# Scaling the attention probabilities with two-tensor products on VectorE, the inverse row sum repeated along the columns

## The reference, cut to what matters

```
q = einsum('bsd,hed->bhse', x, W_Q);  k, v likewise
scores = einsum('bhse,bhme->bhsm', q, k) * scale
scores = where(causal, -1e9, scores)
pattern = softmax(scores, axis=-1)
z = einsum('bhsm,bhme->bhse', pattern, v)
out = einsum('bhse,hde->bsd', z, W_O)
```

## Time and profile before

| | |
|---|---|
| time, median of 3 runs | 1674.98 us (1674.21 to 1677.10) |
| the profiled execution, its time | 1677.12 us |
| its span (first to last instruction) | 1675.2 us |
| TensorE busy | 1617.7 us, 97% |
| VectorE busy | 1140.4 us, 68% |
| ScalarE busy | 767.0 us, 46% |
| GpSimd busy | 627.3 us, 37% |
| TensorE's granted clock | 0.995 of full speed |

### The profile page before, as it was taken

One profiled execution on the slowest core, in us unless ns is written; L12 is line 12 of the kernel. 1 busy time (PEld: TensorE's weight loads), 2 busy tenths in 40 slices (PEclk: granted clock), 3 DMA queues, 4 the chain that ended last, 5 costly groups with the idle time before them and its releaser, 6 DMA issues.

```text
span 1675.2 us, 29756 instructions
## 1 busy us (share of the span) xinstructions
PE 1617.7 (97%) x9992; PEld 1414.1 (84%) x9992; DVE 1140.4 (68%) x2889; ACT 767.0 (46%) x1897; POOL 627.3 (37%) x379
## 2 busy tenths in 40 slices
PE   7999999999999889999999999999999999999997
PEld 6988888898888878888888888888888888888886
DVE  5878878787887765556567578748784857753633
ACT  5666666665665543435333444335333533323221
POOL 2322223232222004323467225841675147533232
PEclk9999999999999999999999999999999999999999
DMA  6434434344342026657665556655655466555663
GB/s 214 156 139 142 153 116 175 138 141 153 126 166 110 1 90 200 191 186 214 200 214 181 172 186 206 196 186 158 205 185 175 146 194 196 177 179 175 191 207 107
DMA packets 101498, 278.28 MB, mean 166 GB/s; under 512 B 13488, under 2 KB 17584, under 8 KB 100368
## 3 DMA queue, kind: packets, MB, share of 16 engines
q1 hardware_dynamic: 101392, 276.91, 51.2%
HBM read 230.23 MB, written 46.63 MB: 165 GB/s over the span
## 4 chain that ended last, share of the span: by engine, by line
PE 59%; DVE 15%; issue 15%; POOL 6%; ACT 4%; DMA 1%; SPq 0%; POOLq 0%; DVEq 0%; ACTq 0%
PE psum L334 53%; POOL act_sb L551 4%; PE psum L1293 2%; DVE s_sb L991 1%; PE psum L1304 1%; DVE conv L1098 1%; POOL mix L573 1%; DVE act_lo L1057 1%; ACT p_sb L674 1%; PE psum L1480 1%; PE psum L1283 1%; ACT kT_hi L633 1%; DVE s_sb L989 1%; DVE kT_lo L885 1%; DVE stats L892 1%
## 5 line engine op out<-in xcount | busy, mean ns | idle before, releaser
L334 PE MATMUL psum<-xT_hi,gu_w 128*128 128x512 f32 x1632 | 554.5, 400 | 1.3 <-DVE act_sb L1052 1.1
L551 POOL TENSOR_TENSOR act_sb<-act_sb,comb 128x512 f32<-128x512 f32 x184 | 310.2, 1686 | 627.6 <-DVE act_sb L1052 627.4
L714 ACT ACTIVATE gated<-psum 128x512 f32<-128x512 f32 x204 | 122.0, 598 | 618.9 <-PE psum L334 618.7
L1052 DVE TENSOR_TENSOR act_sb<-psum,gated 128x512 f32<-128x512 f32 x204 | 140.7, 690 | 380.9 <-PE psum L334 379.4
L334 PEld LDWEIGHTS psum<-xT_hi,gu_w 128*128 128x128 f32 x1632 | 307.7, 189 | 73.7 <-DVE act_sb L1052 3.0
L334 PE MATMUL psum<-xT_lo,gu_w 128*128 128x512 f32 x816 | 322.9, 396 | 0.0
L334 PEld LDWEIGHTS psum<-d_w,act_hi 128*128 128x128 f32 x1632 | 221.8, 188 | 18.6 <-issue 0.6
L517 POOL TENSOR_TENSOR split_stage<-raw_stage,split_stage 128x768 fp32r<-128x768 f32 x56 | 103.0, 1839 | 354.2 <-ACT split_stage L623 354.2
L334 PE MATMUL psum<-d_w,act_hi 128*128 128x256 f32 x1632 | 227.3, 282 | 0.4 <-ACT act_hi L722 0.4
L334 PEld LDWEIGHTS psum<-xT_lo,gu_w 128*128 128x128 f32 x816 | 153.9, 189 | 29.7
L1057 DVE TENSOR_TENSOR act_lo<-act_sb,act_hi 128x512 fp32r<-128x512 f32 x204 | 150.4, 737 | 1.8 <-ACT act_hi L722 1.8
(11 more groups left out here) (203 smaller groups left out, 3502.8 us busy)
## 6 DMA issues: line engine op xcount, KB each, us to landing
gu_w<-w_split SPq DMA_DIRECT2D x204, 512.0 KB, 3.6
d_w<-w_split SPq DMA_DIRECT2D x204, 256.0 KB, 3.8
w_split<-split_stage SPq DMA_DIRECT2D x56, 768.0 KB, 3.9
raw_stage<-w_all SPq DMA_DIRECT2D x56, 384.0 KB, 4.3
decay_all<-decay_dram SPq DMA_DIRECT2D x32, 384.0 KB, 5.2
in_w<-w_split SPq DMA_DIRECT2D x44, 256.0 KB, 4.1
aw_raw<-attn_w SPq DMA_DIRECT2D x8, 1024.0 KB, 6.3
comb<-l_comb_dram SPq DMA_DIRECT2D x128, 64.0 KB, 3.1
```

Source lines behind the costliest of these rows:

```text
L334: last = nc.tensor.matmul(out_ap, w, m, start=start and n == 0, stop=stop and n == len(pairs) - 1, **kw)
L551: pool.tensor_tensor(act_sb[:, s % 2, :], act_sb[:, s % 2, :], comb[:, comb_block(s) % 2, :], ALU.mult).then_inc(comb_done, 1)
L714: act.activation(gated[:, s % 2, :], psum[:, G_BANK, :], ACT.Silu).then_inc(gated_ready, 1)
L1052: dve.tensor_tensor(act_sb[:, s % 2, :], psum[:, U_BANK, :], gated[:, s % 2, :], ALU.mult).then_inc(t_ready, 1)
```

## The change

Both scaling instructions become a product of two tensors. The second tensor is the column of inverse row sums, read again for each column. Before, the same column was a per-partition scalar of a one-tensor operation. The number of instructions, their order, their semaphores and the values computed are the same on every engine.

```
--- before.py
+++ after.py
@@ -995,8 +995,8 @@
                         dve.wait_ge(p_ready, g * UNITS + u + 1)
                         dve.reciprocal(row_inv[:, u % 3, :], row_sum[:, u % 3, :]).then_inc(r_ready, 1)
                         dve.wait_ge(r_ready, g * UNITS + u + 1)
-                        dve.tensor_scalar(p_sb[:, u % 3, 0:P], p_sb[:, u % 3, 0:P], row_inv[:, u % 3, 0:1], None, ALU.mult)
-                        dve.tensor_scalar(p_sb[:, u % 3, P:3 * P], p_sb[:, u % 3, P:3 * P], row_inv[:, u % 3, 1:2], None,
+                        dve.tensor_tensor(p_sb[:, u % 3, 0:P], p_sb[:, u % 3, 0:P], row_inv[:, u % 3, 0:1].to_broadcast([P, P]), ALU.mult)
+                        dve.tensor_tensor(p_sb[:, u % 3, P:3 * P], p_sb[:, u % 3, P:3 * P], row_inv[:, u % 3, 1:2].to_broadcast([P, 2 * P]),
                                           ALU.mult).then_inc(p_scaled, 1)
```

## The result

The changed kernel takes 1678.65 us in the median of 20 runs (1677.36 to 1680.41), against 1675.90 for 20 runs of the kernel before. The ratio is 1.0018 with a 95% interval of 1.0011 to 1.0025. By the ratio that is 3.0 us slower, from 1.8 to 4.2; the two medians lie 2.75 us apart. The forecast was 1677.9 from a median of 1674.98, 2.9 us slower.

What follows compares the result with a forecast made beforehand. TensorE, busy 97% of the span, was taken as the bound, VectorE counting only where TensorE waits. 0.14 + 0.13 + 0.14 = 0.41 us a group over 7 groups gave 2.9 us, 1677.9 us; 8-in-10 range 1674.6 to 1682.3.

Steps and rivals of the forecast that it cites:

- The free product: VectorE's scaling while GpSimd doesn't hold it: 128 columns stay at 0.29 us, a pair occupies VectorE 0.07 us longer.
- The held product: Scaling started while GpSimd runs: still held, 128 columns end about 0.07 us later behind it, a held unit costs 0.14 more.
- The other rate: Factor 1.87 on the 256-column scaling's whole 0.26 us: 0.49 us, summing to 6 us or 1681.
- free units: Units GpSimd doesn't hold: their 0.07 us is swallowed by a following wait, cost nothing; uncovered, 5 us.
- Units 0, 10 and 12: Held units with less room before TensorE waits: 0.14, 0.13 and 0.14 us, 0.41 us a group over 7 groups.
- The term of unit 10: Double hold, the 256-column scaling running after GpSimd's end: 0.13 us; up to 0.07 more if GpSimd's next instruction waits.
- TensorE's waits at the transposes: In each group with splits, TensorE's waits before the transposes were to grow by 0.13 us each.
- the list of signs: Expected trace marks: 256-column scaling at 415 to 425 ns, group 73.2 us, transpose waits 0.13 longer, later rows only shifted.
- Its own range: The forecast's spread over the attention: 2.0 us (unit 12's 0.05 and half of unit 0 absorbed) to 3.8 us.
- All hidden: Another late chain takes over where TensorE's waits end: 1675.0 us, no change; chance 0.17.
- Every held unit counts: Holds lengthen and use up the 0.20 us of room, so all held units reach TensorE: 7.8 us, 1682.8; chance 0.2.
- The hold goes away: GpSimd doesn't hold the product in the scaling: 9.8 us faster, 1665.2, at most 15.4, 1659.6; chance 0.05.

Runs made afterwards that it cites:

- the odd kernel: Product form only in the odd units, old scaling in the even ones, against the kernel before: 1675.07 us, ratio 0.9998.
- the even kernel: Product form only in the even units, old scaling in the odd ones, against the kernel before: 1678.16 us against 1676.11, ratio 1.0017.
- the two one-line kernels: Kernel before with only the 128-column scaling made a product: 1677.66 us (1.0011); with only the 256-column one: 1678.40 us (1.0015).
- the 128-column fill: Changed kernel plus a fill of 128 spare columns behind the 256-column scaling in even units: 1681.33 us against 1674.84 for the kernel before (1.0033).
- the 384-column fill: Changed kernel plus a fill of 384 spare columns behind the 256-column scaling in even units: 1690.95 us against 1675.67 for the kernel before (1.0093).
- the kernel with the accumulator: Kernel before with its one-tensor scaling also writing a sum to a spare column, in all units: 1666.52 us against 1674.84 (0.9939).
- the kernels without holds: GpSimd's splits cut to 8 columns per part, old scaling or products: 1664.14 and 1664.18 us against 1674.84; or old scaling with accumulator: 1666.52.
- the last experiment: Changed kernel plus a 384-column fill behind the 256-column scaling in even units: 1690.95 us against 1675.67 for the kernel before (1.0093).

## Why the prediction was right

**The free product** was priced at 0.29 us and 0.07 us more for 256 columns, from a product with a repeated column and one with an operand in PSUM. It measured 293 ns and 416 against 346.

**The held product** was the step on which the sign hung. That a product with a repeated column is held was read off L959 and is confirmed by 57 long L998. They end 0.147 us behind GpSimd's instruction in the median, against 0.084 before. The prediction counted 56 held units and put the eighth group at nothing; the one that is held there changes nothing in its sum. The other rate that the prediction weighed is a factor of 1.87, an estimate from the figures of the Trainium skill (VectorE: DVE Perf Modes, § The perf-mode tier table), which it took for L999 as a whole. This case doesn't follow it at 256 columns: free, L999 lets its successor start after 0.34 us (206.96 to 207.30 in the changed kernel) where it was 0.26, not after 0.49, and the kernel lost 3.0 us instead of 6.

**Where it counts.** Nothing for free units: shown by the odd kernel (0.9998). Units 0, 10 and 12 of seven groups: shown by the even kernel, by the two one-line kernels that add up to 0.46, and by the 128-column fill. The terms were 0.14, 0.13 and 0.14. They came out as 0.14, 0.19 and 0.14, less 0.02 behind unit 15. The term of unit 10 was too small by 0.05, because the product keeps GpSimd's next instruction waiting; the prediction had named that as up to 0.07 and left it out. The sum of 0.45 x 7 = 3.2 us less an eighth group 0.3 shorter makes the 2.9 of the trace, and that this meets the forecast's 2.9 to the digit is luck. The prediction expected TensorE's waits at the transposes to grow by 0.13 each: the one at unit 10 grew by 0.18, the one at unit 14 not at all, since behind unit 14's hold `qT_first` waits for ScalarE's `qT_hi`. In the kernel before it starts 0.49 us after L999 (230.57 to 231.06) where 0.26 would do, in the changed one 0.41 (231.00 to 231.41) where 0.34 would do, so the pause took up the 0.14. The sum had it right (unit 14 isn't in it), the list of signs had not. Nor were all rows behind the attention the same, only later: the clock differed there.

**The range.** Its own range of 2.0 to 3.8 us around 1674.98 is 1677.0 to 1678.8, and with the scatter of the runs that the prediction names, 0.8 and 2.1 us, it is 1676.2 to 1680.9. The 1676.5 to 1679.5 it gives are neither. The measured time lies in each of them.

**The rivals.** All hidden (0.17): no, the ratio's interval excludes 1. Every held unit counts (0.2): no, with 0.14 us late a group would be 1.1 us longer; but the 384-column fill shows the overrun that it spoke of, once a held unit is 0.49 us late. The hold goes away (0.05): no for this form. Its price agrees: 9.8 to 15.4 us was forecast for a kernel without holds, and 10 and 11 us were measured by the ratios, in two ways. In part that is luck. The 9.8 us took both waits for `pT_lo` as gone, 1.4 us a group. They fell by 1.1, and a group gained 1.5: by the starts of L996 of the kernel with the accumulator 0.3 behind unit 0, which the 9.8 us left out, 0.7 behind unit 10 and 0.5 behind unit 12. The 0.8 us for `kT_lo` that the upper figure rested on doesn't go, since it is a round trip over ScalarE and not the hold.

What stays open is why the wait for `pT_lo` behind unit 14 keeps 0.3 us in the kernels without holds, where unit 14 is free too, and which held unit's delay lands behind unit 12 and which behind 14 in the last experiment.

## What to carry to other kernels

Look for instructions of one form with two very different durations in the trace, and lay the other engine's timeline beside them before pricing a change of the form: here an instruction of 290 ns cost 649 in the mean, and the form decides whether it is held. Price a form change per place: the same 0.07 us cost nothing in 64 units and everything in three. When a form is held, look for one that isn't even if it is slower by itself; 476 ns instead of 346, never held, made the kernel 10 us faster.

## What the runs showed of the hardware

- VectorE's scaling is held until GpSimd's running instruction ends, in both forms. It ends 0.08 us (old form) or 0.15 us (product) after it for 128 columns, 0.15 or 0.28 for 256, as medians over the 57 L998 and the 7 L999 of either kernel. The form with an accumulator, 345 to 348 ns for 128 columns, is not: 64 of its 128 ran inside one instruction of GpSimd.
- The hold works the other way too: GpSimd's 128x512 `aw_lo`, started while a held product was finishing, took 1.34 to 1.35 us against 1.28 to 1.30 with the old form.
- A fill of 128 columns lasts 165 ns in the record and delayed what came behind it by 0.08 us; one of 384 lasts 378 and delayed by 0.35.
- TensorE's granted clock was 0.66 in 5 us behind a 2.6 us pause in one execution and 1.00 in another of nearly the same program, which shifted what follows by 1.4 us, nearly half of the effect measured here. Spans of single executions should not be compared for effects of this size.
